# Seven block products in place of eight for a head pair's projections, block sums on GpSimd, buffers laid out anew

## The chip, the cores and the metric

The kernel runs on one core of a Trainium2 chip. The metric is the device time of one execution in microseconds. TensorE (PE) multiplies into PSUM; VectorE (DVE) and ScalarE (ACT) move results out of PSUM; GpSimd (POOL) works on SBUF only; transfers are issued by the queues of SyncE (SP), ACT and POOL. Each engine works through its own instructions in order, and waits on semaphores for the others.

## The reference, cut to what matters

A decoder block with three parts: a gated linear attention, a product with quantised operands, and a small block-diagonal feed-forward, each added to its input and normalised. The attention takes most of the time. In the reference it runs over blocks of 64 rows with a carried state; the kernel computes the same as one masked product over 512 rows, with a decay matrix.

```python
qkv = jax.nn.silu(hidden_states @ qkv_w.T)       # hidden: (2, 512, 1024), 32 heads of 128
scores = jnp.einsum('bhnd,bhmd->bhnm', cq, ck) * diag_decay
intra = jnp.einsum('bhnm,bhmd->bhnd', scores, cv)
...
xf = xf * jax.lax.rsqrt(jnp.mean(xf * xf, axis=-1, keepdims=True) + EPS)
normed = norm_w * xf.astype(attn.dtype)
gate = jax.nn.sigmoid(hidden_states @ gate_w.T)
return gate * normed @ out_w.T
```

Every float32 operand of these products is split into a high and a low float16 part, and a product is three: high x high, high x low, low x high.

## The kernel before, in words

`make_plan` writes one list of steps; five functions, one for each engine, walk that list and emit their part of each step. The order of the list is therefore the order of each engine's queue. Buffers are handed out by `Ring` objects that remember which semaphore value frees a slot.

The 32 heads form 16 groups of two. Groups 0 to 11 are worked for both batches in one block; groups 12 to 15 (`TAIL_GROUPS = 4`) once for batch 0 and then once for batch 1, so that batch 0's later stages run under batch 1's attention. In a block, each unit (a head h and a batch b) has these steps:

- `project` for q, k and the gate: 8 k-tiles of 3 matmuls of 128x512 into one bank (lines 779 to 781), 24 in all. For q and k, ACT takes the sigmoid of the bank (L947), DVE multiplies (L1074), ACT writes the high half (L950), DVE the low half (L1035): four turns of two engines. For the gate, ACT takes the sigmoid (L942).
- `project_v`, once for a group, a batch and 128 rows: 24 matmuls of 128x256 (L792 to L794), then the same four turns at half width.
- `scores`: 12 matmuls through the helper `three` (L762); DVE multiplies by the decay (L1087), ACT and DVE write the halves (L956, L1035), one bank after the other.
- `attend`: 12 matmuls (L817 to L819) into the one bank of `aring`; ACT squares (L962), DVE multiplies by norm weight and gate (L1100), ACT and DVE write the halves (L965, L1035), and DVE adds the square to `ssq` (L1106).
- `out_product` of the group before, for a batch and 128 rows: two halves of 6 matmuls each (L762), which DVE adds to `acc` (L1115).

Weights come by DMA from SP, 512 KB at a time, into five buffers `raw`; ACT writes the high half (L932) and DVE the low half (L1035). `between` inserts such steps between the projections. After the attention come `rows_phase` (residual, norm, quantised product) and `ffn_phase`.

## Time and profile before

| what | value |
|---|---|
| median of three runs | 2164.41 us (2163.93 to 2165.61) |
| the profiled execution | 2164.81 us, of which the span is 2162.9 us |
| PE busy | 2028.4 us (94%) |
| DVE busy | 1272.9 us (59%) |
| ACT busy | 816.1 us (38%) |
| POOL busy | 119.1 us (6%) |
| mean granted clock of TensorE | 0.97 |

Read it so: the page's share of busy time is a mean over the span; the table of stretches gives it by stage, with the granted clock beside it. Matmuls overlap each other in their records (one lasts longer than the step from one to the next), so what PE needs for a piece of work is read from the starts of the first and of the next piece in the timeline, not from durations. In a timeline row the first number is the start, the second the time to the end of the group of merged instructions, and in brackets stands how long the engine had been idle and who released it.

### The profile page before, as it was taken

How to read it: one execution, taken by the hardware profiler on the slowest of the kernel's cores; microseconds unless marked ns; L12 is line 12 of the kernel's file. 1: busy time of each engine (PE TensorE's matmuls, PEld its weight loads, DVE VectorE, ACT ScalarE, POOL GpSimd, SP SyncE). 2: the span in 40 equal slices, each digit the busy share in tenths (PEclk: the TensorE clock that was granted, in tenths of full speed). 3: DMA queues.
4: the chain of work that ended last, by engine and by line, in shares of the span. 5: the costliest groups of instructions: out<-in, count | busy, mean ns of one | idle time of the engine just before them, and what ended most of it. 6: DMA issues, size and time to landing. Idle time of an engine off the chain costs nothing.

```text
span 2162.9 us, 29130 instructions
## 1 busy us (share of the span) xinstructions
PE 2028.4 (94%) x11455; PEld 1098.8 (51%) x11464; DVE 1272.9 (59%) x1966; ACT 816.1 (38%) x1360; POOL 119.1 (6%) x132
## 2 busy tenths in 40 slices
PE   7999999999999999999999999999999899986654
PEld 4464646455564646464645555455555445542211
DVE  5655555555555555555555556556666666667887
ACT  4432323242323233332323233333444434444763
POOL 0000000000000000000000000000000000004465
PEclk9999999999999999999999999999999999997877
DMA  5120202020201102120202022123323322323311
GB/s 196 44 74 35 74 35 74 13 96 1 98 10 40 69 35 73 35 74 35 74 24 84 1 98 69 38 104 108 108 80 138 117 96 104 106 83 103 93 55 58
DMA packets 54071, 154.02 MB, mean 71 GB/s; under 512 B 5936, under 2 KB 14256, under 8 KB 53936
## 3 DMA queue, kind: packets, MB, share of 16 engines
q1 hardware_dynamic: 41056, 135.28, 17.8%
q0 software_dynamic: 3840, 12.59, 1.9%
q10 hardware_dynamic: 9040, 4.29, 0.7%
q8 instruction: 92, 1.51, 0.3%
q14 instruction: 43, 0.35, 0.1%
HBM read 143.75 MB, written 8.39 MB: 70 GB/s over the span
## 4 chain that ended last, share of the span: by engine, by line
PE 78%; DVE 11%; ACT 4%; issue 3%; DMA 2%; SPq 1%; POOL 1%; POOLq 0%; ACTq 0%; DVEq 0%
PE bank L762 18%; PE bank L781 14%; PE bank L780 14%; PE bank L779 14%; PE bank L792 4%; PE bank L794 4%; PE bank L793 4%; PE bank L817 1%; PE bank L819 1%; PE bank L818 1%; DVE x_split L1178 1%; DMA raw<-w_qk 1%; DVE w_head L1035 1%; DVE w_out_group L1183 1%; DVE bank L1087 1%
## 5 line engine op out<-in xcount | busy, mean ns | idle before, releaser
L779 PE MATMUL bank<-x_split,w_head 128*128 128x512 f16 x1536 | 582.7, 379 | 0.2 <-DVE v_split L1035 0.2
L780 PE MATMUL bank<-x_split,w_head 128*128 128x512 f16 x1536 | 582.6, 379 | 0.0
L781 PE MATMUL bank<-x_split,w_head 128*128 128x512 f16 x1536 | 582.4, 379 | 0.0
L762 PE MATMUL bank<-w_out_group,gated_split 128*128 128x512 f16 x1536 | 344.6, 385 | 20.8 <-DVE acc L1115 11.0
L947 ACT ACTIVATE sig<-bank 128x256 f32<-128x256 f32 (+1 forms) x256 | 124.8, 487 | 563.1 <-PE bank L781 496.9
L1074 DVE SCALAR_TENSOR_TENSOR bank<-bank,sig 128x256 f32<-128x256 f32 (+1 forms) x256 | 144.3, 564 | 273.7 <-ACT sig L947 272.3
L792 PE MATMUL bank<-w_v_group,x_split 128*128 128x256 f16 x1024 | 281.8, 275 | 18.9 <-DVE x_split L1035 11.4
L794 PE MATMUL bank<-w_v_group,x_split 128*128 128x256 f16 x1024 | 281.7, 275 | 0.0
L793 PE MATMUL bank<-w_v_group,x_split 128*128 128x256 f16 x1024 | 281.7, 275 | 0.0
L762 PEld LDWEIGHTS bank<-w_out_group,gated_split 128*128 128x128 f16 x1536 | 151.2, 99 | 209.1 <-issue 26.2
L781 PEld LDWEIGHTS bank<-x_split,w_head 128*128 128x128 f16 x1536 | 150.4, 98 | 181.3 <-issue 0.3
L779 PEld LDWEIGHTS bank<-x_split,w_head 128*128 128x128 f16 x1536 | 150.6, 98 | 169.3 <-DVE v_split L1035 0.5
L780 PEld LDWEIGHTS bank<-x_split,w_head 128*128 128x128 f16 x1536 | 150.4, 98 | 168.7
L1115 DVE TENSOR_TENSOR acc<-acc,bank 128x512 f32<-128x512 f32 x240 | 160.0, 685 | 86.4 <-PE bank L762 86.1
L1035 DVE SCALAR_TENSOR_TENSOR w_head<-raw,w_head 128x1024 f16<-128x1024 f32 x120 | 146.4, 1225 | 86.3 <-ACT w_head L932 86.1
L956 ACT ACTIVATE scores_split<-bank 128x512 f16<-128x512 f32 (+1 forms) x192 | 100.9, 526 | 249.7 <-DVE bank L1087 249.7
L1035 DVE SCALAR_TENSOR_TENSOR scores_split<-bank,scores_split 128x512 f16<-128x512 f32 (+1 forms) x192 | 115.8, 603 | 114.6 <-ACT scores_split L956 114.6
L1087 DVE TENSOR_TENSOR bank<-bank,decay_sb 128x512 f32<-128x512 f32 (+3 forms) x256 | 119.8, 491 | 34.9 <-PE bank L762 34.9
L932 ACT ACTIVATE w_head<-raw 128x1024 f16<-128x1024 f32 x120 | 125.4, 1051 | 37.8 <-DMA raw<-w_qk 37.6
L762 PE MATMUL bank<-q_split,k_split 128*128 128x512 f16 (+3 forms) x768 | 116.1, 302 | 2.7 <-DVE k_split L1035 2.7
L792 PEld LDWEIGHTS bank<-w_v_group,x_split 128*128 128x128 f16 x1024 | 100.9, 99 | 33.8 <-issue 10.0
L794 PEld LDWEIGHTS bank<-w_v_group,x_split 128*128 128x128 f16 x1024 | 101.1, 99 | 12.6
(172 smaller groups left out, 1987.6 us busy)
## 6 DMA issues: line engine op xcount, KB each, us to landing
raw<-w_qk SPq DMA_DIRECT2D x80, 512.0 KB, 4.6
raw<-w_v SPq DMA_DIRECT2D x40, 512.0 KB, 7.5
raw<-w_gate SPq DMA_DIRECT2D x40, 512.0 KB, 6.2
raw<-w_out SPq DMA_DIRECT2D x40, 512.0 KB, 4.5
decay_sb<-decay SPq DMA_DIRECT2D x40, 256.0 KB, 2.7
raw<-ctx_in SPq DMA_DIRECT2D x16, 512.0 KB, 4.6
acc<-x_t SPq DMA_DIRECT2D x8, 512.0 KB, 9.7
raw<-x_n SPq DMA_DIRECT2D x8, 512.0 KB, 4.2
```

What stands on the lines that cost most here:

```text
L762: last = pe.matmul(out, a, b, start=m == 1, stop=m == n)
L779: pe.matmul(bank[:, :], wt[:, j, 0, k], x[:, 0, k], start=k == 0, stop=False)
L780: pe.matmul(bank[:, :], wt[:, j, 0, k], x[:, 1, k], start=False, stop=False)
L781: mm = pe.matmul(bank[:, :], wt[:, j, 1, k], x[:, 0, k], start=False, stop=k == KT - 1)
L792: pe.matmul(out, x[:, 0, k, cols], c.w_vg[:, 0, k], start=k == 0, stop=False)
L793: pe.matmul(out, x[:, 0, k, cols], c.w_vg[:, 1, k], start=False, stop=False)
L794: mm = pe.matmul(out, x[:, 1, k, cols], c.w_vg[:, 0, k], start=False, stop=k == KT - 1)
L932: act.activation(hi, src, ACT.Copy, scale=scale).then_inc(sem["w_hi"])
L1035: return dve.scalar_tensor_tensor(out=lo, in0=src, scalar=scale, in1=hi, op0=ALU.mult, op1=ALU.subtract)
L1074: dve.scalar_tensor_tensor(out=ps, in0=ps, scalar=1.0 / W_SCALE, in1=c.sig32[st["gi"]][:, 0:n], op0=ALU.mult, op1=ALU.mult).then_inc(sem[" ...
L1087: ins = dve.tensor_tensor(ps, ps, c.decay_sb[slot][:, 0:n], ALU.mult)
L1115: dve.tensor_tensor(dst, dst, bank[:, :], ALU.add).then_inc(sem["acc"])
```

## The change

For groups 0 to 12 (`MAIN = 13`) the q, k and gate projections of a head pair are treated as a product of 2x2 blocks: two heads by two halves of the hidden size, times two halves by two batches. A block product is 4 k-tiles of 3 matmuls of 128x512. Instead of eight such products for each of q, k and gate, seven are made, of sums of blocks (the scheme of Winograd). What comes with it:

- The seven blocks of x are made once at the start: sums and differences of 128x2048 on DVE (`x_t1`, `x_t3`) and POOL (`x_t2`, `x_t4`), then a high and a low half of each (ACT and DVE, 128x2048 each). x arrives in four transfers of 1 MB.
- The weights of a pair arrive in one transfer of 1 MB into one of two buffers. POOL makes three block sums (and one in place) with four additions of 128x512 (`pair_sum`). ACT and DVE write the halves of 7 blocks of 512 columns in three parts, 1024, 1024 and 1536 wide (`pair_split`), where before there were two of 1024 for each of the three.
- The results are built up in PSUM. Product 1 goes to bank 0, ACT copies bank 0 to bank 1 (`seed`), and product 2 goes on in bank 0, product 6 in bank 1. Product 7 goes to bank 2 and ACT copies it to SBUF (`copy_p7`, `s7`). DVE adds bank 1 and `s7` into bank 2 (`u3`); product 5 goes on in bank 1; DVE adds bank 1 and `s7` into `s7` (`c22`); product 4 goes on in bank 2, product 3 in bank 1. The order on PE is 1, 7, 2, 6, 5, 4, 3. The four results are the four units of the pair; unit 3 is read from SBUF.
- v is still made with all its matmuls, but for a second batch the first half of k uses the block `b0 - b1`: ACT copies the first partial result (`v_copied`), DVE subtracts (`v_sub`), and PE waits for both.
- The scores, attends and out products of group n-1 are placed by hand into the products of group n: all scores and attends lie in the gate's products (the fourth attend in q's), all out products in q's, and the four v tiles in k's. The decays of the scores are taken one ahead of the low halves.
- The addition to `ssq` goes from DVE to POOL for these groups.
- `TAIL_GROUPS` is 3, and the steps from the main part to the tail are written out. The tail's own steps are as before; `between` advances `rows_phase` twice at a time, the second batch's x block is loaded again (`x12`), and most buffers of the tail are views of the main part's.

```diff
...
+PRODUCTS = {1: (0, 0, 0), 2: (1, 1, 0), 3: (6, 3, 1), 4: (3, 6, 2), 5: (2, 2, 1), 6: (4, 4, 1), 7: (5, 5, 2)}
...
+    def product(self, i):
...
+        free = {1: self.bank_free[0], 7: self.bank_free[2], 2: self.t_seeded, 6: self.t_seeded, 5: self.t_u3,
+                4: self.t_u3, 3: self.t_c22}[i]
...
+    plan.split_pair(0)
+    for name in ("x_t1", "x_t3", "x_t2"):
+        plan.add(name)
+        plan.tick(name)
+    for i, block in enumerate(X_ORDER):
+        plan.x_split(block)
+        if i == 0:
+            plan.split_pair(1)
+        if i == 1:
+            split_pair(2)
+        if block == 1:
+            plan.add("x_t4", split=plan.x_block[1])
+            plan.tick("x_t4")
+    plan.add("quant_consts")
+
...
+        fill("p1-")
+        plan.product(1)
+        fill("p1")
+        plan.seed()
+        fill("p7-")
+        plan.product(7)
+        plan.copy_p7()
+        fill("p7")
+        plan.product(2)
+        out(0)
+        fill("p2")
+        plan.product(6)
+        plan.add_u3()
+        fill("p6")
+        plan.product(5)
+        plan.add_c22()
+        out(3)
+        fill("p5")
+        plan.product(4)
+        fill("p4")
+        out(2)
+        plan.product(3)
+        fill("p3")
+
...
+        product_pair("gate", n, {
...
+            "p1-": [score(0)],
+            "p1": [part(0)],
+            "p7": [attend(0), score(1)],
+            "p2": [part(1)],
+            "p6": [attend(1), score(2)],
+            "p5": [part(2)],
+            "p4": [attend(2), score(3)],
+            "p3": [split_vo],
+        })
+        product_pair("q", n, {
+            "p1": gate_last if first else [attend(3)] + gate_last,
+            "p7": [part(0)],
+            "p6": [part(1)] if first else out(0, 1, 2, 3) + [part(1)],
+            "p5": [] if first else out(4, 5),
+            "p4": [part(2)] if first else [part(2)] + out(6, 7),
+            "p3": [lambda: plan.qk_out("q", 1)] + ([] if first else out(8, 9, 10, 11, 12, 13, 14, 15)),
+        })
+        if not first:
+            plan.load_decay(n * GH)
+            plan.load_decay(n * GH + 1)
+        product_pair("k", n, {
+            "p1": [split_vo],
+            "p2": [part(0)],
+            "p6": [lambda: plan.v_pair(0)],
+            "p5": [part(1)],
+            "p3": [lambda: plan.qk_out("k", 1), part(2), lambda: plan.v_pair(1), lambda: plan.v_pair(2),
+                   lambda: plan.v_pair(3)],
+        })
...
+    plan.main_scores(last_n, UNITS[0])
+    plan.finish_loads(plan.idle, ("head", g0 * GH))
+    plan.project(g0 * GH, 0, 0)
+    plan.main_attend(last_n, UNITS[0])
+    plan.main_scores(last_n, UNITS[1])
+    plan.prefetch_v(g0)
+    plan.project(g0 * GH, 0, 1)
...
+            i, wp = st["i"], st["wp"]
+            block, x, place = PRODUCTS[i]
+            bank, fresh = c.banks[place], i in (1, 7)
+            until(pe, sem, st["free"])
+            until(pe, sem, st["x"])
+            pe.wait_ge(sem["w_lo"], st["w"][1])
+            for k in range(QT):
+                w_hi, w_lo = (c.wp[:, wp, n, block, k * P:(k + 1) * P] for n in range(2))
+                x_hi, x_lo = (c.xb[:, x, n, k, :] for n in range(2))
+                pe.matmul(bank[:, :], w_hi, x_hi, start=fresh and k == 0, stop=False, skip_group_check=not fresh)
+                pe.matmul(bank[:, :], w_hi, x_lo, start=False, stop=False, skip_group_check=not fresh)
+                mm = pe.matmul(bank[:, :], w_lo, x_hi, start=False, stop=k == QT - 1, skip_group_check=not fresh)
...
+            pe.wait_ge(sem["v_copied"], st["copied"][1])
...
+            pe.wait_ge(sem["v_sub"], st["sub"][1])
...
+            act.activation(c.banks[1][:, :], c.banks[0][:, :], ACT.Copy).then_inc(sem["seeded"])
...
+            act.activation(c.s7[:, :], c.banks[2][:, :], ACT.Copy).then_inc(sem["p7_copied"])
...
+            dve.tensor_tensor(bank[:, :], c.banks[1][:, :], c.s7[:, :], ALU.add).then_inc(sem["u3"])
...
+            dve.tensor_tensor(c.s7[:, :], c.banks[1][:, :], c.s7[:, :], ALU.add).then_inc(sem["c22"])
...
+            until(pool, sem, st["free"])
+            pool.wait_ge(sem[st["landed"][0]], st["landed"][1])
+            pool.tensor_tensor(s3, a11, a21, ALU.add)
+            pool.tensor_tensor(a21, a21, a22, ALU.add).then_inc(sem["pair_sum"])
+            pool.wait_ge(sem["pair_sum"], st["s1"][1])
+            pool.tensor_tensor(s2, a11, a21, ALU.add).then_inc(sem["pair_sum"])
+            pool.wait_ge(sem["pair_sum"], st["s2"][1])
+            pool.tensor_tensor(s4, a12, s2, ALU.add).then_inc(sem["pair_sum"])
+        elif kind == "x_t2":
...
+            pool.tensor_tensor(c.ssq[:, b], c.ssq[:, b], c.square_of(st), ALU.add).then_inc(sem["ssq_pool"])
...
```

## Rows read from the trace of the kernel before

**Rows 1.** Table of stretches: us, each engine's busy time (instructions), clock, DMA share, GB/s.
```profile
1150.00:1200.00 50.00, 50.00 (x346) 33.22 (x345) 25.15 (x44) 18.68 (x37) 0.00 (x0) 1.00 0.23 80
```

**Rows 2.** Timeline of PE, group 4: start, us, engine line op, names, count.
```profile
613.25 1.79 PE L762 MATMUL bank<-q_split,k_split 128*128 128x512 f16 x12
614.88 0.38 PE L779 MATMUL bank<-x_split,w_head 128*128 128x512 f16 x1
...
620.06 2.11 PE L762 MATMUL bank<-w_out_group,gated_split 128*128 128x512 f16 x9
```

**Rows 3.** Timeline of ACT: sigmoids of the last two v tiles at the start.
```profile
36.79 0.38 ACT L947 ACTIVATE sig<-bank 128x256 f32<-128x256 f32 x1 [1.35 <-PE bank L794]
...
39.41 0.38 ACT L947 ACTIVATE sig<-bank 128x256 f32<-128x256 f32 x1 [1.36 <-PE bank L794]
```

**Rows 4.** Timeline of DVE: one addition of half an out product.
```profile
637.09 0.69 DVE L1115 TENSOR_TENSOR acc<-acc,bank 128x512 f32<-128x512 f32 x1 [0.61 <-PE bank L762]
```

**Rows 5.** Timeline of ACT: first v sigmoid of two successive groups.
```profile
596.22 0.38 ACT L947 ACTIVATE sig<-bank 128x256 f32<-128x256 f32 x1
...
713.19 0.38 ACT L947 ACTIVATE sig<-bank 128x256 f32<-128x256 f32 x1
```

**Rows 6.** Timelines of ACT and DVE: the four turns of one q.
```profile
646.16 0.60 ACT L947 ACTIVATE sig<-bank 128x512 f32<-128x512 f32 x1 [23.41 <-PE bank L781]
646.79 0.70 DVE L1074 SCALAR_TENSOR_TENSOR bank<-bank,sig 128x512 f32<-128x512 f32 x1 [5.12 <-ACT sig L947]
647.52 0.60 ACT L950 ACTIVATE q_split<-bank 128x512 f16<-128x512 f32 x1 [0.77 <-DVE bank L1074]
648.15 0.69 DVE L1035 SCALAR_TENSOR_TENSOR q_split<-bank,q_split 128x512 f16<-128x512 f32 x1 [0.66 <-ACT q_split L950]
```

**Rows 7.** Groups of instructions by line: busy us, mean ns, idle before.
```profile
L1035 DVE SCALAR_TENSOR_TENSOR w_head<-raw,w_head 128x1024 f16<-128x1024 f32 x120 | 146.4, 1225 | 86.3 <-ACT w_head L932 86.1
L932 ACT ACTIVATE w_head<-raw 128x1024 f16<-128x1024 f32 x120 | 125.4, 1051 | 37.8 <-DMA raw<-w_qk 37.6 <-DMA raw<-w_gate 0.2
```

**Rows 8.** Timelines of ACT and DVE: square and low half of one attend.
```profile
690.79 0.59 ACT L962 ACTIVATE square<-bank 128x512 f32<-128x512 f32 x1
...
692.95 0.69 DVE L1035 SCALAR_TENSOR_TENSOR gated_split<-bank,gated_split 128x512 f16<-128x512 f32 x1 [0.66 <-ACT gated_split L965]
```

**Rows 9.** Timeline of DVE: later decays of one unit's scores.
```profile
660.84 0.76 DVE L1087 TENSOR_TENSOR bank<-bank,decay_sb 128x384 f32<-128x384 f32 x2
...
662.86 0.42 DVE L1087 TENSOR_TENSOR bank<-bank,decay_sb 128x256 f32<-128x256 f32 x1
```

**Rows 10.** Timelines of DVE and ACT at the start: splits of x.
```profile
13.44 7.31 DVE L1035 SCALAR_TENSOR_TENSOR x_split<-acc,x_split 128x512 f16<-128x512 f32 x12
18.09 1.15 ACT L936 ACTIVATE x_split<-acc 128x512 f16<-128x512 f32 x2 [0.20 <-DMA acc<-x_t]
```

**Rows 11.** Timelines of POOL and DVE in the feed-forward stage.
```profile
2049.33 1.06 POOL L1247 TENSOR_TENSOR square<-acc 128x512 f32<-128x512 f32 x1
...
2051.54 1.27 POOL L1252 TENSOR_TENSOR sig<-sig,square 128x512 f32<-128x512 f32 x1
2048.98 4.39 DVE L1178 TENSOR_TENSOR x_split<-w_head,x_split 64x512 f16<-64x512 f32 x1
```

**Rows 12.** Timeline of PE: the stop where both-batch blocks end.
```profile
1328.37 11.81 PE L762 MATMUL bank<-w_out_group,gated_split 128*128 128x512 f16 x54 [1.42 <-DVE acc L1115]
```

**Rows 13.** Timeline of PE, two stops, and the stretches behind each.
```profile
1931.03 1.19 PE L762 MATMUL bank<-q_split,k_split 128*128 128x512 f16 x3 [2.74 <-DVE k_split L1035]
1932.00:1934.00 2.00, 2.00 (x11) 1.30 (x10) 0.92 (x3) 1.01 (x1) 0.00 (x0) 0.50 0.23 23
1934.00:1936.00 2.00, 2.00 (x9) 0.83 (x8) 0.76 (x1) 1.17 (x3) 0.00 (x0) 0.81 0.65 242
1942.76 0.38 PE L817 MATMUL bank<-scores_split,v_split 128*128 128x512 f16 x1 [2.20 <-issue]
1942.00:1944.00 2.00, 1.24 (x7) 0.71 (x8) 0.57 (x2) 2.00 (x4) 0.00 (x0) 1.00 0.00 0
```

747 lines of the change are left out of this document (598 added, 149 removed).

## The prediction

> **What bounds the kernel now.** I read the table of stretches first. In the main part PE is busy for all 50 us of a 50 us stretch at granted clock 1.00 (the full level of 2.4 GHz), DVE for about half [rows 1]. Then the waits of PE: between 60 and 1300 us that view is empty. So in groups 0 to 11 only matmuls cost time; every wait that the change adds to PE there counts in full, and so does every matmul that it takes away.
>
> What PE needs, from starts in the timelines: a projection of 24 matmuls takes 620.06 - 614.88 = 5.18 us, so 0.216 us a matmul and 2.59 us for a block product of 12. Scores take 614.88 - 613.25 = 1.63 us, an attend with the same column counts as much [rows 2]. A v tile takes 39.41 - 36.79 = 2.62 us [rows 3]; half an out product 0.69 + 0.61 = 1.30 us [rows 4]. A group: 12 x 5.18 + 8 x 2.62 + 8 x 1.63 + 16 x 1.30 = 117 us, and the same step recurs after 713.19 - 596.22 = 117.0 us [rows 5]. PE has no slack.
>
> **Matmuls removed.** 3 kinds x 12 matmuls = 36 a group, 36 x 0.216 = 7.8 us, for 13 groups -101 us. A group then needs 117.0 - 7.8 = 109.2 us of PE. This is sure; the question is what is given back.
>
> **The steady group (1 to 12).** Prices: the four turns of a q or k result start 0.63, 0.73, 0.63 us apart (sigmoid, product, high half, low half; the last slot 0.61), 2.6 us together, because each engine waits for the other [rows 6]. A low half of 1024 takes 1.23 us on DVE and the high half 1.05 on ACT; 0.69 and 0.60 are those of 512 [rows 6, 7], so 1536 is estimated at 1.76 and 1.5. An attend holds DVE from its gate product on for 0.75 + 0.6 + 0.7 = 2.0 us, 2.8 us after the square begins [rows 8]. A score block is 0.68 and 0.35 [rows 9] and 0.61 [rows 10] of decays and as much of low halves, 3.3 us on DVE in the new order. I lay these behind each other in the written order, PE's start of the gate's products being 0:
> - Gate part. PE has 7 x 2.59 + 7 x 1.63 = 29.5 us. DVE has 4 x 3.3 of scores, 3 x 2.0 of attends, 4.0 of splits, 1.3 of `u3` and `c22`, and 1.9 left over from the last v tile, plus waits for ACT: it falls behind. The low halves of the fourth scores come at 32.8, PE wants the fourth attend at 32.1: 0.8 us.
> - q part. ACT's order is `split_vo`, square, high half, `gate_out(1)`, `seed`. The fourth attend ends on PE at 34.6; DVE comes from `split_vo` at 36.0; gate product, high half, gate and seed follow to 38.4. Product 2 waits for the seed from 37.2: 1.3 us. Here and in k, out products and v tile 0 cover `u3`, and product 4 covers `c22`.
> - End of the k part. Products 5, 4 and 3 follow each other without filler, and three results with two parts of a split go through ACT and DVE in turns. With T the end of product 3 on PE: `c22` from T-5.0, unit 3 until T-1.7, the split of part 1 until T-0.1, unit 2 until T+1.8, unit 1's high half until T+3.2, the 1536-wide high half until T+4.6, and only then ACT's copy of v tile 1, until T+4.9. PE wants it at T+2.6 and stops for 2.4 us; then `v_sub` is late by another 0.4, behind the 1536-wide low half.
>
> Together 0.8 + 1.3 + 2.4 + 0.4 = 4.9 us, and 0.5 for the starts after four stops: 5.4 us of 7.8. For 12 groups +65 us. No row shows these stops. Bounds: 3.0 us (only the k part) gives +36, 7.5 (a third more of everything) +90. I take 5.4, since each of its turns has a row of the same shape. No gain is possible here: PE had no wait to lose.
>
> **Group 0 and the start.** In the q and k parts of group 0 nothing fills the places: `u3` stands open (1.2), bank 2 is late (0.6), the k end as above: +5 us (3 to 7). At the start the kernel of before has its first v products done at 39.4 us for 8 x 2.62 = 21.0 us of work [rows 3]: 18.4 us lost. The last 512 KB of x land at about 18 us [rows 10], after 5 MB as in the change. In the change ACT's seed of the first product stands in its queue behind the high halves of all seven x blocks. Block 6 waits for `x_t4` on POOL, and that for block 1's low half. A DVE pass of 2048 is estimated at 2.3 us (0.61 per 512 in a row [rows 10], 1.23 per 1024), one of POOL at 4.9 (1.22 to 1.27 per 512 [rows 11]). DVE: `x_t1` 12.8 to 15.1, `x_t3` to 17.8, then block 0, part 1, block 5, part 2, block 1 to 27.2; `x_t4` to 32.3; high halves of 6 and 3 to 36.1; seed 36.7. Five products, `u3` and a half clock at first (below) end at 53; ideal is 18.1. Lost 35, that is +17. With POOL and DVE excluding each other, as next, it ends at 61: +25. I take +21, bounds 14 and 28.
>
> **POOL beside DVE.** At 2048.98 a DVE operation with both inputs in SBUF, 0.69 us otherwise, takes 4.39: POOL's operations run back to back until 2052.8 and DVE ends 0.56 us behind them [rows 11]. Under the same burst DVE operations with an input in PSUM kept their length. The pair's sums are bursts of 4 x 1.27 = 5.1 us, three a group; what can be hit are the weight splits and unit 3. By my layout one burst meets q's part 0 split (5 us of out products cover it), the others run beside v tiles and out additions, whose inputs are in PSUM. In the steady group 0. The Trainium skill, page "SBUF — State Buffer", section "Who interferes with whom", says that a VectorE instruction with two SBUF inputs and a GpSimd one that reads SBUF exclude each other for a whole instruction. The row agrees, and goes further: POOL's operations in a row held DVE out. By the rule alone, with one operation of 1.27 a hit and two hits a group, the sum would be at most 12 x 2.5 = 30 higher, and only where nothing covers the split.
>
> **From main part to tail.** After the last v tile PE has one score block (1.6 us), then waits for three splits: DVE's scores end at 5.1, three low halves at 9.1: 7.6 us idle. The v weights' splits stand behind the third attend and fourth scores: about 6.5. The out weights' splits stand behind the v tiles: about 3. Sum 17, and 4 for the clock: +21 (14 to 26). The before had one stop of 1.4 us at its own passage [rows 12], which goes: -1.4.
>
> **The tail.** The second batch's part, under which batch 0's row steps and the context hide, is one block shorter; its extra work is the same. -5 to +12, I take +4. Transfers are no bound: a pair's 1 MB has about 30 us.
>
> **The clock.** The stop of 2.74 us was followed by the level of 1.2 GHz: after 2.74 us of idle, 2 us at 0.50 and 2 us at 0.81 lose 1.4 us, with what lay before them some 1.7; after 2.20 us the clock stayed at 1.00 [rows 13]. The new stop of 2.4 us lies between. I take it as mostly unhurt, +3 us in all (0 to 22).
>
> **Sum.** -101 + 65 + 5 + 21 + 21 - 1.4 + 4 + 3 = +16.6. 2162.9 + 16.6 = 2179.5 of span; the execution was 1.9 us longer than its span, and it stands 0.4 us above the median of the runs: 2181 us, 0.8% slower.
>
> **The rivals.**
> - The k end is not late (faster). Mechanism and place: ACT's copy of v tile 1. It decides at 2.6 us behind product 3. If the chain of turns runs 2.4 us ahead of my layout, because unit 3 and part 1 are done before product 4 ends, then 2.8 us a stop vanish 13 times, the 3 us of clock too: 2181 - 39 = 2142. With the gate part's stops gone as well (2.1 x 12), 2117. For it: in the rows of before the same turns never stop PE, and a part of my durations overlaps in the records. Against: in before no two results came closer than 5.18 us, here 2.59. Chance 0.28.
> - The clock falls at every k end (slower). 13 x 1.7 = 22 in place of 3, and 3 to 5 in the start: 2203. For it the 2.74 us row, against it the 2.20 one. Chance 0.14.
> - POOL's bursts reach the gate part. If a pair's sums start beside the third or fourth scores, a split is held for what is left of 5.1 us, some 3 on average, with no cover [rows 11]; 12 x 3 = 36: 2217. Against: they stand in POOL's queue behind the fourth `ssq`. Chance 0.08.
> - The change doesn't do what it says: matmuls that go on in a bank written by ACT or DVE step slower than 0.216. No row shows such a bank. At 0.22 it would be 13 x 180 x 0.004 = 9 us: 2190. Chance 0.02.
> - The forecast as worked out: 0.48, its own range 2160 to 2200.
>
> **How the numbers follow.** The likeliest case gives 2181. The range takes the first rival's nearer time with room, 2130, and the POOL rival's, 2217. About 0.2% (4 us, to 2160 and 2169) is what a measurement of this kernel can tell from no change. Faster takes the first rival and a little of the forecast's low bounds: 0.30. The same: 0.11. Slower: 0.59.
>
> **What would show it.** In the changed kernel PE's waits from 100 to 1400 us must name three places, the attend behind the fourth scores, the seed before product 2, and ACT's copy and DVE's difference in v tile 1, with 5 us a group together and a period near 114.5 us. A period under 111 speaks for the first rival. Clock rows of 0.5 to 0.9 once a group speak for the clock, DVE splits of 3 to 6 us in the gate part for POOL. The first group's products should end at 53 to 61 us. The prediction is wrong if PE hardly waits there, or if the passage to the tail costs far from 20 us.

## The result and the profile after

The changed kernel takes 2178.28 us (median of 4 runs, 2176.79 to 2179.55), the kernel before 2164.17 us beside it (2162.66 to 2165.61): a ratio of 1.0065, 95% interval [1.0048, 1.0082]. It is slower by 0.65%. The profiled execution has a span of 2176.8 us, 13.9 more than before, and a mean granted clock of 0.962.

The matmuls did go. The page of the changed kernel, instructions and busy time of each engine:

```profile
PE 1955.0 (90%) x10988; PEld 1057.4 (49%) x10997; DVE 1388.8 (64%) x2068; ACT 934.5 (43%) x1512; POOL 434.0 (20%) x342
```

PE has 10988 matmuls where it had 11455: 467 fewer (13 x 36 = 468, one record may be missing), and is busy for 90% of the span where it was for 94%. What it lost is in the waits. Waits of PE, changed kernel, whole span (us in total, times, longest), and in a second block the same view from 200 to 1300 us, where the kernel before has no wait at all:

```profile
PE bank L1220 <- ACT bank L1447: 28.2, 14, 11.1
PE bank L1246 <- ACT sig L1460: 25.0, 12, 2.1
```

```profile
PE bank L1246 <- ACT sig L1460: 20.9, 10, 2.1
PE bank L1220 <- ACT bank L1447: 12.2, 9, 1.4
PE bank L1312 <- issue: 4.7, 9, 0.5
PE bank L1253 <- DVE bank L1616: 1.4, 4, 0.4
```

L1246 is the third of the four stages of a v tile (it waits for ACT's copy, L1460), L1253 the fourth (for DVE's difference, L1616), L1220 a product (for the seed, L1447), L1312 an attend. They stand at fixed places of each group. Timeline of PE, changed kernel, one group: start, us, what ran, and in brackets the idle time before it and its releaser:

```profile
223.57 0.28 PE L1246 MATMUL bank<-w_vo,x_blocks 128*128 128x256 f16 x1 [2.09 <-ACT sig L1460]
225.42 0.40 PE L1253 MATMUL bank<-w_vo,x_blocks 128*128 128x256 f16 x1 [0.26 <-DVE bank L1616]
...
271.39 0.38 PE L1312 MATMUL bank<-scores_split,v_split 128*128 128x512 f16 x1 [0.52 <-issue]
...
277.13 0.39 PE L1220 MATMUL bank<-x_blocks,w_pair 128*128 128x512 f16 x1 [1.36 <-ACT bank L1447]
...
339.05 0.28 PE L1246 MATMUL bank<-w_vo,x_blocks 128*128 128x256 f16 x1 [2.09 <-ACT sig L1460]
...
1373.38 0.28 PE L1246 MATMUL bank<-w_vo,x_blocks 128*128 128x256 f16 x1 [2.09 <-ACT sig L1460]
```

The same stop recurs after 339.05 - 223.57 = 115.5 us. In group 0 it is at 108.31, in group 11 at 1373.38: (1373.38 - 108.31) / 11 = 115.0 us a group, where it was 117.0 [rows 5] and 109.2 of matmuls are left.

Why the v tile waits is on ACT and DVE. Timeline of ACT ahead of that stop, changed kernel (the 1536-wide row is part 2 of the next pair's split), then the two rows of DVE:

```profile
219.80 0.59 ACT L1465 ACTIVATE sig<-bank 128x512 f32<-128x512 f32 x1
221.27 0.60 ACT L1470 ACTIVATE k_units<-bank 128x512 f16<-128x512 f32 x1 [0.87 <-DVE bank L1620]
221.76 1.47 ACT L1432 ACTIVATE w_pair<-sums_pair 128x1536 f16<-128x1536 f32 x1
223.14 0.38 ACT L1460 ACTIVATE sig<-bank 128x256 f32<-128x256 f32 x1
...
223.27 1.76 DVE L1570 SCALAR_TENSOR_TENSOR w_pair<-sums_pair,w_pair 128x1536 f16<-128x1536 f32 x1 [0.68 <-ACT w_pair L1432]
224.94 0.42 DVE L1616 TENSOR_TENSOR bank<-sig,bank 128x256 f32<-128x256 f32 x1
```

ACT has unit 1's turn and then part 2 ahead of the copy (L1460), with no idle time but the 0.87 in which it waits for DVE inside the turn. The copy ends at 223.52; PE starts at 223.57. The clock is the other thing that appears. Table of stretches, changed kernel (length, then PE, PEld, DVE, ACT, POOL busy, clock, DMA share, GB/s), behind the stops of two successive groups:

```profile
224.00:226.00 2.00, 1.74 (x13) 1.13 (x12) 1.75 (x3) 0.38 (x1) 0.89 (x1) 0.70 0.00 0
226.00:228.00 2.00, 2.00 (x12) 1.41 (x10) 0.47 (x2) 0.39 (x1) 1.92 (x3) 0.50 0.89 262
228.00:230.00 2.00, 2.00 (x19) 1.76 (x18) 0.86 (x2) 1.15 (x3) 1.92 (x2) 0.95 0.64 262
...
342.00:344.00 2.00, 2.00 (x21) 1.79 (x19) 1.00 (x3) 1.03 (x3) 1.92 (x2) 1.00 0.94 350
```

After the same 2.09 us of idle the level of 1.2 GHz (0.50) appears in one group and not in the next. It appears after 8 of the 12 stops. A period that begins with a fall is 115.3 to 115.5 us long, one without is 114.1, so a fall costs 1.1 to 1.4 us here. The clock itself loses more in the three rows, 0.30 x 2 + 0.50 x 2 + 0.05 x 2 = 1.7 us; part of that is covered, because behind a fall PE comes to DVE's difference later and waits for it less or not at all, where it waits 0.37 us in a group without a fall.

The start and the passage to the tail. Timeline of PE, changed kernel: the first products, and the passage:

```profile
23.21 0.61 PE L1220 MATMUL bank<-x_blocks,w_pair 128*128 128x512 f16 x1 [20.33 <-DVE x_blocks L1570]
...
42.15 0.61 PE L1220 MATMUL bank<-x_blocks,w_pair 128*128 128x512 f16 x1 [11.09 <-ACT bank L1447]
...
1507.62 0.58 PE L1274 MATMUL bank<-x_blocks,w_pair 128*128 128x512 f16 x1 [7.46 <-DVE w_pair L1570]
1541.28 0.37 PE L1287 MATMUL bank<-w_vo,x_blocks 128*128 128x256 f16 x1 [6.22 <-DVE w_vo L1570]
```

11.09 us is the wait for the first seed, behind the x splits. The third gap of the passage is 3.07 us (at 1560.42).

So the 101 us of removed matmuls, and 14 more, were given back in four places: steady stops, the start, the passage and the clock. What the runs had to settle is whether each stop is what the prediction said it is: an engine's queue ahead of one operation, which can be reordered, or a chain that has to be that long.

### The profile page after: what moved, and what is told of

It is laid out like the page before. It is cut to its first block, busy times and chain, and to the rows that moved or that the text cites. A ratio compares the mean times of both kernels' runs of the same rounds, so it can differ in the third digit from the quotient of the medians.

```text
span 2176.8 us, 29088 instructions
## 1 busy us (share of the span) xinstructions
PE 1955.0 (90%) x10988; PEld 1057.4 (49%) x10997; DVE 1388.8 (64%) x2068; ACT 934.5 (43%) x1512; POOL 434.0 (20%) x342
## 4 chain that ended last, share of the span: by engine, by line
PE 73%; DVE 14%; ACT 6%; issue 5%; DMA 1%; POOL 1%; SPq 0%; ACTq 0%; POOLq 0%; DVEq 0%
PE bank L1197 18%; PE bank L1220 10%; PE bank L1222 10%; PE bank L1221 10%; PE bank L1274 2%; PE bank L1276 2%; PE bank L1275 2%; DVE w_pair L1570 2%; PE bank L1312 2%; ACT w_pair L1432 1%; PE bank L1314 1%; PE bank L1313 1%; DVE x_blocks L1570 1%; PE bank L1253 1%; PE bank L1254 1%
## 5 line engine op out<-in xcount | busy, mean ns | idle before, releaser
L1220 PE MATMUL bank<-x_blocks,w_pair 128*128 128x512 f16 x1092 | 415.8, 381 | 51.9 <-ACT bank L1447 28.2
L1221 PE MATMUL bank<-x_blocks,w_pair 128*128 128x512 f16 x1092 | 415.7, 381 | 0.0
L1222 PE MATMUL bank<-x_blocks,w_pair 128*128 128x512 f16 x1092 | 415.5, 381 | 0.0
L1197 PE MATMUL bank<-w_vo,gated_split 128*128 128x512 f16 x1152 | 256.5, 379 | 0.0
L1833 POOL TENSOR_TENSOR ssq<-ssq,sig 128x512 f32<-128x512 f32 x52 | 86.0, 1654 | 575.1 <-ACT sig L1497 575.1
L1220 PEld LDWEIGHTS bank<-x_blocks,w_pair 128*128 128x128 f16 x1092 | 107.2, 98 | 181.0 <-ACT bank L1447 35.1
L1570 DVE SCALAR_TENSOR_TENSOR w_pair<-raw_pair,w_pair 128x1024 f16<-128x1024 f32 x108 | 141.5, 1317 | 71.6 <-ACT w_pair L1432 58.5
L1620 DVE SCALAR_TENSOR_TENSOR bank<-bank,sig 128x256 f32<-128x256 f32 (+1 forms) x182 | 99.2, 545 | 135.0 <-ACT sig L1465 134.4
L1814 POOL TENSOR_TENSOR sums_pair<-raw_pair 128x512 f32<-128x512 f32 x39 | 51.6, 1323 | 645.8 <-DVE w_pair L1570 400.3
L1197 PEld LDWEIGHTS bank<-w_vo,gated_split 128*128 128x128 f16 x1152 | 112.7, 98 | 135.9
L1222 PEld LDWEIGHTS bank<-x_blocks,w_pair 128*128 128x128 f16 x1092 | 107.2, 98 | 130.0 <-issue 1.9
L1465 ACT ACTIVATE sig<-bank 128x256 f32<-128x256 f32 (+1 forms) x182 | 86.2, 474 | 191.4 <-PE bank L1248 112.7
L1221 PEld LDWEIGHTS bank<-x_blocks,w_pair 128*128 128x128 f16 x1092 | 107.2, 98 | 119.6 <-issue 1.8
L1491 ACT ACTIVATE scores_split<-bank 128x512 f16<-128x512 f32 (+1 forms) x192 | 100.7, 526 | 119.3 <-DVE bank L1673 115.3
L1274 PE MATMUL bank<-x_blocks,w_pair 128*128 128x512 f16 x288 | 112.0, 389 | 15.7 <-DVE w_pair L1570 15.7
L1276 PE MATMUL bank<-x_blocks,w_pair 128*128 128x512 f16 x288 | 111.7, 388 | 0.0
L1275 PE MATMUL bank<-x_blocks,w_pair 128*128 128x512 f16 x288 | 111.6, 388 | 0.0
L1197 PE MATMUL bank<-k_units,gated_split 128*128 128x512 f16 x384 | 89.7, 393 | 13.5 <-DVE acc L1705 6.2
L1570 DVE SCALAR_TENSOR_TENSOR w_pair<-sums_pair,w_pair 128x1536 f16<-128x1536 f32 (+1 forms) x45 | 75.8, 1684 | 37.3 <-ACT w_pair L1432 35.7
```

What stands on the lines that cost most here:

```text
L1197: last = pe.matmul(out, a, b, start=m == 1, stop=m == n)
L1220: pe.matmul(bank[:, :], w_hi, x_hi, start=fresh and k == 0, stop=False, skip_group_check=not fresh)
L1221: pe.matmul(bank[:, :], w_hi, x_lo, start=False, stop=False, skip_group_check=not fresh)
L1222: mm = pe.matmul(bank[:, :], w_lo, x_hi, start=False, stop=k == QT - 1, skip_group_check=not fresh)
L1274: pe.matmul(bank[:, :], wt[:, j, 0, k], x_hi, start=k == 0, stop=False)
L1275: pe.matmul(bank[:, :], wt[:, j, 0, k], x_lo, start=False, stop=False)
```

## Experiments

Each starts from the changed kernel ("p4" is the place behind product 4 in the list of a projection's fillers, and so on); `...` marks cut lines. Ratios are against the kernel before, and "less" or "more" is against the changed kernel's 2178.28 us. The theory: the k end's stop is ACT's queue ahead of v tile 1's copy; the gains and losses of the places add up. Its rival: the stop is a chain that moves but does not shrink.

**k_end: v tile 1 ahead of unit 1's turn.**

```diff
-            "p3": [lambda: plan.qk_out("k", 1), part(2), lambda: plan.v_pair(1), lambda: plan.v_pair(2),
-                   lambda: plan.v_pair(3)],
+            "p3": [lambda: plan.v_pair(1), lambda: plan.qk_out("k", 1), part(2), lambda: plan.v_pair(2),
+                   lambda: plan.v_pair(3)],
```

> At the end of each k part v tile 1 is placed ahead of unit 1's result and of part 2 of the split; nothing else changes. Order theory (the stop of 2.09 us at v tile 1 and the 0.37 behind it come from ACT's place in its queue, and the half clock in two of three groups from the length of that stop): ACT's copy of v tile 1 then follows unit 2's high half at 1.2 us behind product 3 and is in time, both stops go, the clock stays at 1.00, and the period falls from 115.26, 115.48, 114.13 us to about 111.6 in every group. 13 x (2.1 + 0.3) + 9 x 1.25 = 43 us less than 2178: 2135 us. Rival (GpSimd's sums delay VectorE and through it the k end): the stop keeps most of its length, 2165 us or more. Rival (matmuls in banks that ACT or DVE wrote are slower): no change, 2178.

Measured 2179.43 us, ratio 1.0057 [1.0037, 1.0078]: no gain, a miss. The trace shows where the stop went. Timelines of ACT and then PE, k_end:

```profile
226.45 0.59 ACT L1465 ACTIVATE sig<-bank 128x512 f32<-128x512 f32 x1
227.81 0.60 ACT L1470 ACTIVATE k_units<-bank 128x512 f16<-128x512 f32 x1 [0.77 <-DVE bank L1620]
228.30 1.48 ACT L1432 ACTIVATE w_pair<-sums_pair 128x1536 f16<-128x1536 f32 x1
229.67 0.38 ACT L1460 ACTIVATE sig<-bank 128x256 f32<-128x256 f32 x1
...
230.10 0.28 PE L1246 MATMUL bank<-w_vo,x_blocks 128*128 128x256 f16 x1 [2.23 <-ACT sig L1460]
```

These are the same three pieces of work, now ahead of v tile 2's copy, and PE stops for 2.23 us one tile later. The queue was the cause, but I had moved it, not shortened it: v tiles follow each other without a filler, so whatever stands between two of their copies stops PE. The time alone, 2179, would also have fitted the rival in which matmuls are slower in banks that ACT or DVE wrote. The starts of the products in the changed kernel rule that out: products 5 and 4 of a gate part, in such banks, take 262.26 - 257.08 = 5.18 us, products 1 and 7, in fresh banks, 245.38 - 240.20 = 5.18.

**k_split_late: part 2 of the split behind the last v tile.**

```diff
-            "p3": [lambda: plan.qk_out("k", 1), part(2), lambda: plan.v_pair(1), lambda: plan.v_pair(2),
-                   lambda: plan.v_pair(3)],
+            "p3": [lambda: plan.qk_out("k", 1), lambda: plan.v_pair(1), lambda: plan.v_pair(2),
+                   lambda: plan.v_pair(3), part(2)],
```

> Only part 2 of the split is moved, behind all four v tiles; unit 1's result stays ahead of v tile 1. This tells which turn in the chain is dear. The copy of v tile 1 then comes after unit 1's high half, 3.6 us behind product 3 in place of 4.9: the stop falls from 2.1 to about 0.8 and the clock no longer falls: 13 x 1.7 + 9 x 1.25 = 33 us gained. But the 1.76 us of VectorE and then GpSimd's sums of the next pair move to the beginning of the gate part, where by the layout VectorE has no slack: the stop at the fourth attend grows from 0.5 to 2.3, and q's part 0 split may wait for a burst. 12 x 1.8 to 12 x 2.8 lost. Net -11 to 0: 2167 to 2178 us. If VectorE has slack in the gate part after all, 2145.

Measured 2157.92 us, ratio 0.9957 [0.9943, 0.9971]: 20.4 us less than the changed kernel, and faster than before. Waits of PE from 200 to 1300 us, k_split_late:

```profile
PE bank L1312 <- issue: 9.6, 20, 0.5
PE bank L1246 <- ACT sig L1460: 7.2, 10, 0.7
```

The stop fell from 2.09 to 0.72, by 1.37 (part 2's slot on ACT is 223.14 - 221.76 = 1.38). The difference's wait is gone. Two small stops are new (0.39 for part 2's low half, 0.43 for an attend). The clock stays at 1.00 in this run's groups. The period is 113.4, from 115.0: 1.6 x 12 = 20, nearly the whole gain. The time lies between the two that I gave: the k end did what was expected, but my main case had the fourth attend's stop grow to 2.3 us by DVE's extra 1.76 us, and it stayed at 0.53. At the beginning of the gate part DVE had room for that piece.

**ssq_dve: the addition of the squares back on DVE.** In the branch of DVE for an attend, and the same taken out of POOL's:

```diff
             if "unit" in st:
+                dve.wait_ge(sem[st["ssq_before"][0]], st["ssq_before"][1])
+                dve.tensor_tensor(c.ssq[:, b], c.ssq[:, b], c.square_of(st), ALU.add).then_inc(sem["ssq_pool"])
                 continue
...
```

> Undoes one part of the change: the addition to ssq of groups 0 to 12 is VectorE's again. Order theory with VectorE as the one that sets the gate part: 0.61 us more for each of four attends there, of which some 0.6 are absorbed by slack before the second and third attend; the stop at the fourth attend grows from 0.5 by about 1.5 and q's seed stays where it is behind it: 12 x 1.5 to 12 x 2.2, so 2196 to 2205 us. Rival (the GpSimd addition holds the splits, its mean is 1.65 us against 1.27 alone, so moving it costs as much as it saves): 2178 or less.

Measured 2222.20 us, ratio 1.0250 [1.0233, 1.0267]: 44 us more, beyond both. Waits of PE from 200 to 1300 us, ssq_dve; then the split of v's and out's weights on DVE in one group, in the changed kernel and in ssq_dve, and POOL beside the latter:

```profile
PE bank L1220 <- ACT bank L1447: 28.0, 9, 3.5
PE bank L1312 <- issue: 15.1, 9, 1.7
```

```profile
272.25 2.36 DVE L1570 SCALAR_TENSOR_TENSOR w_vo<-raw_pair,w_vo 128x1024 f16<-128x1024 f32 x2 [0.96 <-ACT w_vo L1437]
...
277.44 4.25 DVE L1570 SCALAR_TENSOR_TENSOR w_vo<-raw_pair,w_vo 128x1024 f16<-128x1024 f32 x2 [0.96 <-ACT w_vo L1437]
280.70 2.13 POOL L1821 TENSOR_TENSOR sums_pair<-raw_pair,sums_pair 128x512 f32<-128x512 f32 x1
```

The k end's stop is as it was (2.09). The attend's stop grows from 0.52 to 1.67, by 1.15, the direction and nearly the size that was expected (about 1.5): three of the four additions stand ahead of the fourth scores in DVE's queue. What I had wrong is the seed, which was to stay: its stop grows from 1.36 to 3.1 in the mean. The rows say why. The pair's sums on POOL now meet `split_vo` on DVE, whose two pieces take 4.25 us together in place of 2.36. In the group in which one piece alone is held (1.22 and 2.29 us, at 396.56) the seed's stop is 2.43; in the group shown, with both held, it is 3.25, and 3.25 - 1.36 = 1.89 is the time for which POOL held the two. So of the 2.9 us a group, 35 in 12, more than half comes from POOL holding DVE and not from the additions' own length; the rest of the 44 us is not worked out, but behind the seed's stop the clock now falls too in some groups (0.50 from 286 to 288 us), for which I had no term. This is the prediction's rival of POOL's bursts; in the changed kernel the additions of squares on POOL stood ahead of the sums and kept them off that split.

**eight: product 4 made twice.** 12 more matmuls a projection, so as many as before, everything else as in the changed kernel. The output is not the reference's: block 3's product counts twice.

```diff
-            for k in range(QT):
+            for m in range(QT * (2 if i == 4 else 1)):
+                k, last = m % QT, m == QT * (2 if i == 4 else 1) - 1
...
```

> Product 4 is made twice in each of the 39 pairs' products, which puts back the number of matmuls of an eighth product (the result is then not the reference's). 39 x 2.59 = 101 us of matmuls more. Order theory: during 2.59 us more of cover the copy of v tile 1 and q's fourth scores catch up, so the stops at the k end (2.4), the clock falls (0.85 a group on average) and most of the stops at the fourth attend (0.5) and the seed (1.4) go: 13 x 3.2 + 12 x 1.9 = 65 us come back, 2178 + 36 = 2214 us, so an eighth of the products costs a third of its price. Rival (the stops are independent of cover): 2279 us.

Measured 2240.48 us, ratio 1.0339 [1.0321, 1.0356]: 62 us more for 101 us of matmuls, between the two: 39 us came back where I expected 65. The period went from 115.0 to 119.7, 7.8 of matmuls and -3.1 of the rest: the attend's 0.52 is gone, the seed's 1.36 is 0.81, the v tile's 2.09 is 1.08, and the clock does not fall in any of these groups. So the stops are not a fixed price of the new order; part of them is time in which the other engines catch up, and matmuls put there cost less than their length. This measures directly what the seven products bring inside this kernel: 62 us, not 101.

**k_p4: part 2 ahead of unit 2's turn.**

```diff
+            "p4": [part(2)],
-            "p3": [lambda: plan.qk_out("k", 1), part(2), lambda: plan.v_pair(1), lambda: plan.v_pair(2),
+            "p3": [lambda: plan.qk_out("k", 1), lambda: plan.v_pair(1), lambda: plan.v_pair(2),
```

> Whole computation; only the k part's last piece (1536 wide, 1.47 on ACT and 1.76 on DVE) is moved ahead of product 3 of k instead of behind the last unit's silu. If v tile 1 waits for what is queued ahead of its copy on ACT (our theory), product 3's 7.8 us hide the piece together with unit 2's turn, the stop at v tile 1 falls from 2.09 to about 0.7 (only the last unit's turn is left ahead of the copy, as in the variant that put the piece last), the 0.39 that that variant waited for its next weights does not appear, and the clock does not fall: period 115.0 -> about 112.9, some 25 us in all, 2150 to 2156. Rival: the piece now delays unit 2's turn and its sums from GpSimd are not ready there, so that product 3's end meets a longer queue: the stop stays near 2 and the time near 2178.

Measured 2186.16 us, ratio 1.0096 [1.0078, 1.0115]: worse, a miss. The step that failed is the cover: I took 7.8 us for a product; that is three products, one takes 2.59. The stop is 2.62 us, and the clock falls to 0.50 behind 11 of these 12 stops (226 to 228 us in this group). Timeline of PE, k_p4:

```profile
224.85 0.28 PE L1247 MATMUL bank<-w_vo,x_blocks 128*128 128x256 f16 x1 [2.62 <-ACT sig L1461]
```

ACT's order brought nothing while the sum ahead of the copy stayed (k_end, k_p4); the piece has to leave the stretch of products 5, 4 and 3 altogether.

**k_spread: part 2 behind the last v tile, and part 1 out of that stretch too.**

```diff
-            "p6": [lambda: plan.v_pair(0)],
-            "p5": [part(1)],
-            "p3": [lambda: plan.qk_out("k", 1), part(2), lambda: plan.v_pair(1), lambda: plan.v_pair(2),
-                   lambda: plan.v_pair(3)],
+            "p6": [part(1), lambda: plan.v_pair(0)],
+            "p3": [lambda: plan.qk_out("k", 1), lambda: plan.v_pair(1), lambda: plan.v_pair(2),
+                   lambda: plan.v_pair(3), part(2)],
```

> Whole computation; as in the variant that moved k's last piece (1536 wide) behind v tile 3, and the middle piece (1024 wide, 1.04 on ACT, 1.23 on DVE) moved from behind product 5 of k to ahead of v tile 0, where ACT is free for 1.0 and DVE for 6 us. Products last 2.6 us each (12 matmuls x 0.216), so that between the end of product 5 and v tile 1's copy ACT has two units' turns of some 2.1 us each and the middle piece. Theory (the stop at v tile 1 is ACT's queue): without the middle piece unit 2's turn ends a microsecond earlier and the copy follows the last unit's turn alone: the stop 0.72 falls to 0 to 0.1, 13 x 0.7 = 9 us less than the 2157.9 of that variant: 2147 to 2151. Rival: the copy is bound by the last unit's own turn (sigmoid, product, high half, some 2.1 us from the end of product 3), which no other work lengthens: the stop stays 0.7 and the time 2158.

Measured 2146.00 us, ratio 0.9908 [0.9891, 0.9924]: as expected, 1 us below the range given. Waits of PE from 200 to 1300 us, k_spread, and under them its timeline of ACT ahead of the copy:

```profile
PE bank L1219 <- ACT bank L1446: 13.6, 10, 1.4
PE bank L1311 <- issue: 9.5, 20, 0.5
```

```profile
218.14 0.60 ACT L1464 ACTIVATE sig<-bank 128x512 f32<-128x512 f32 x1 [0.47 <-PE bank L1221]
219.50 0.60 ACT L1469 ACTIVATE k_units<-bank 128x512 f16<-128x512 f32 x1 [0.77 <-DVE bank L1619]
220.00 0.38 ACT L1459 ACTIVATE sig<-bank 128x256 f32<-128x256 f32 x1
```

No v tile waits any more (besides these two the view has only the 0.4 us for part 2's low half). ACT now waits for PE (0.47) ahead of unit 1's sigmoid, where in the changed kernel it had none: it has caught up with product 3. The rival, a chain that is bound by the last unit's own turn, falls. Period 112.5.

**start, passage, q_seed: one place each.** Start: the x blocks 6 and 3 are split behind group 0's first `u3` in place of ahead of its seed, and the split of q's first weights follows later.

```diff
-    for i, block in enumerate(X_ORDER):
+    for i, block in enumerate(X_ORDER[:5]):
...
-            "p1": [part(0)],
-            "p2": [part(1)],
-            "p5": [part(2)],
+            "p6": [late_x],
+            "p4": [part(0), part(1)],
+            "p3": [part(2)],
```

> Whole computation; x blocks 6 and 3 are split after group 0's first U3 in place of before the gate products, and q's first two pieces wait for that. Theory: the first seed waits behind those splits on ACT (11.09 us stop at 42.15), so that it comes earlier by the time of two 3.7 us ACT pieces, and part of it is lost again at the later products that read blocks 6 and 3: a gain of 3 to 9 us, 2170 to 2175 where the variant without it has 2178. Rival: GpSimd's sums and VectorE's wide low halves (which take 3.3 in place of 1.27 and 6.6 in place of 2.28 together) set the start whatever their order: 2178 within 2.

Measured 2170.79 us, ratio 1.0028 [1.0018, 1.0038]: 7.5 us less, as expected. The wait of 11.09 us for the seed is gone (3.08 and 2.94 later in its place).

Passage: the loads and splits of the tail's first head weights stand between group 12's v tiles.

```diff
+            "p3": [lambda: plan.qk_out("k", 1), lambda: plan.v_pair(1), tail_loads, tail_head, tail_split,
+                   lambda: plan.v_pair(2), tail_split, lambda: plan.v_pair(3), tail_split],
...
```

> Whole computation; at the end of the last seven-product group the tail's head weights are loaded and split between that group's v tiles instead of behind them. Theory: of the passage's gaps 7.5, 6.2 and 3.1 us the first is the wait for these splits and goes, perhaps some of the second: 6 to 12 us less, 2166 to 2172. Rival: the loads can't start earlier (the buffers that they write are read by products until then), the gap stays: 2178 within 2.

Measured 2169.55 us, ratio 1.0026 [1.0016, 1.0037]: 8.7 us less, as expected. Timeline of PE, passage:

```profile
1503.91 0.38 PE L1289 MATMUL bank<-x_blocks,w_pair 128*128 128x512 f16 x1 [2.02 <-DVE w_pair L1585]
1535.60 0.37 PE L1302 MATMUL bank<-w_vo,x_blocks 128*128 128x256 f16 x1 [6.21 <-DVE w_vo L1585]
```

The first gap is 2.02 us in place of 7.46; the first matmul behind it takes 0.38 where it took 0.58: the granted clock is 1.00 here, and was 0.50 from 1508 to 1510 us in the changed kernel. At the second gap this kernel is 5.7 us ahead; the rest of the gain comes later in the tail, and I have no row that says why.

q_seed: `split_vo` moves from the end of the gate part to behind product 7 of q.

```diff
-            "p3": [split_vo],
+            "p3": [],
...
-            "p7": [part(0)],
+            "p7": [part(0)] if first else [split_vo, part(0)],
```

> Whole computation; the split of v's and out's weights (2 pieces on ACT and DVE) is moved from the end of the gate part to behind product 7 of q, out of the queue ahead of the seed of q. Theory: the stop of 1.36 us ahead of product 2 of q becomes about 0.7 (one gate turn is still ahead of the seed), 12 x 0.65 = 8 us less: 2169 to 2173. Rival: the seed waits for the gate turn alone and the moved pieces now delay the out additions: 2178 or up to 5 us more.

Measured 2176.60 us, ratio 1.0058 [1.0041, 1.0074]: 1.7 us less, which the two intervals don't tell from nothing; 2169 to 2173 was expected, a miss. The seed's stop did halve. Waits of PE from 200 to 1300 us, q_seed, then the moved pieces on DVE and the first out product behind them:

```profile
PE bank L1220 <- ACT bank L1447: 6.1, 9, 0.7
PE bank L1197 <- issue: 4.9, 9, 0.6
```

```profile
275.49 4.37 DVE L1570 SCALAR_TENSOR_TENSOR w_vo<-raw_pair,w_vo 128x1024 f16<-128x1024 f32 x2 [1.92 <-ACT w_vo L1437]
...
279.97 4.26 PE L1197 MATMUL bank<-w_vo,gated_split 128*128 128x512 f16 x19 [0.55 <-issue]
```

The wait of the out products (L1197) is new, 0.55 us. They read the weights that these pieces split, and start 0.1 us behind them. The two pieces take 4.37 us for the 2.36 of the changed kernel, because at their new place they meet the pair's sums on POOL (272.74 to 278.78). With their own length they would have ended 2 us earlier, ahead of the out product: so by these rows what the seed won was lost to POOL.

**all_moves: the four moves together** (k_spread, start, passage, q_seed).

> Whole computation; the moves of the start, of the passage, of v's and out's weight split and of both of k's late pieces together. If each gain is a stop of its own, they add up: 2178.3 - 20.4 (k's last piece) - 9 (the middle one) - 7.5 (start) - 8.7 (passage) - 1.7 (weight split) = 2131, range 2125 to 2140: below the kernel before by 1.2 to 1.8%. Rival: a stop removed at one place comes back at the next (as when v tile 1 was put first): 2145 to 2155.

Measured 2133.26 us, ratio 0.9849 [0.9832, 0.9865]: 1.5% faster than the kernel before, and as expected. The single gains from the changed kernel's 2178.3 are 32.3, 7.5, 8.7 and 1.7, together 50.2; found are 45.0. They add up to within 5 us. Here too the moved pieces of `split_vo` take 4.37 us and the out products wait for 0.55; a run that keeps the pair's sums off them was not made.

**all_moves_vo_early: the out weights' split ahead of q's pair.** In the order of loads `("o", n - 1)` goes ahead of `("q", n)`, and in the gate part:

```diff
-            "p1": [part(0)],
+            "p7-": [split_vo],
             "p7": [attend(0), score(1)],
-            "p2": [part(1)],
-            "p6": [attend(1), score(2)],
+            "p2": [part(0)],
+            "p6": [attend(1), score(2), part(1)],
...
```

> Whole computation; as all moves together, but the out weights are loaded and split ahead of q's pair: their two pieces (2.0 on ACT, 2.36 on DVE) stand behind the gate seed, where DVE was idle for 2.4, and not in q. Theory: the seed of q waits for the gate turn alone (1.36 -> 0.7) and the 0.54 to 0.6 that the out products waited for when the split stood in q don't appear: 12 x 0.6 = 7 us less than all moves: 2124, range 2118 to 2134. Rival: the pieces of q's pair, now later in the gate part, hold up product 1 or 7 of q or the third attend: as all moves or up to 8 us more.

Measured 2153.89 us, ratio 0.9943 [0.9927, 0.9960]: 21 us more than all_moves, far beyond both. Waits of PE from 200 to 1300 us, all_moves_vo_early; then DVE ahead of the first gate product in all_moves, and two rows of DVE in all_moves_vo_early:

```profile
PE bank L1328 <- issue: 28.0, 20, 2.4
```

```profile
237.76 0.76 DVE L1705 SCALAR_TENSOR_TENSOR bank<-bank,norm_w_sb,gate_units 128x512 f32<-128x512 f32 x1 [0.78 <-ACT sig L1514]
...
237.64 2.36 DVE L1586 SCALAR_TENSOR_TENSOR w_vo<-raw_pair,w_vo 128x1024 f16<-128x1024 f32 x2 [0.98 <-ACT w_vo L1453]
...
253.75 1.23 DVE L1586 SCALAR_TENSOR_TENSOR w_pair<-raw_pair,w_pair 128x1024 f16<-128x1024 f32 x1 [0.47 <-ACT w_pair L1448]
```

The fourth attend's stop went from 0.52 to 2.37, and the clock falls behind 7 of the 12. The idle of 2.4 us was a row of the changed kernel (247.84); in all_moves, where k's late piece stands ahead of the gate part, DVE is idle for 0.78 and 0.47 us there. Even so the two pieces of `split_vo` are the lesser part: counted from the first decay, the second gate product comes 14.60 us behind it for 14.31 in all_moves, 0.3 later. The greater part is the last row: q's part 1, which had to make room, stands behind the third scores, where all_moves has no split, and takes 1.7 us of DVE with the idle before it. The fourth scores come 2.0 us later in all. That is the rival as recorded, the pieces of q's pair, at more than twice its price. The out products' wait did vanish, and `split_vo` is not held by POOL (2.36).

**x_sums_dve: the two 2048-wide sums of x on DVE,** on top of all_moves: `x_t2` behind block 0's split and `x_t4` behind the fifth block's, both issued by DVE in place of POOL.

> Whole computation; as all moves together (2133.3), with the two 2048-wide sums of x blocks made on VectorE in place of GpSimd, the first behind block 0's low half, the second behind the fifth block's. Theory: at the start GpSimd and VectorE take turns, not beside each other: GpSimd's 6.5 us sum stands beside block 0's low half, which then takes 6.60 in place of 2.28, and so the first product comes at 23.6. On VectorE the sums cost 2.3 each and nothing waits behind GpSimd: the low half ends 4.3 earlier and the first product starts at 19 to 20; of that 3 to 6 us reach the end of group 0: 2127 to 2130. Rival: the low half is late for another reason (its block's landing, the memory), and 2 x 2.3 more on VectorE lengthen the start: 2134 to 2140.

Measured 2130.77 us, ratio 0.9853 [0.9836, 0.9869], the span of the profiled execution 2127.5. The ratio is that of all_moves, so the gain of 3 to 6 us that was expected is not shown in the whole time; at the start it is. Timelines of POOL and DVE of all_moves, then of DVE and POOL of x_sums_dve:

```profile
14.82 6.54 POOL L1840 TENSOR_TENSOR k_units<-q_units,acc 128x2048 f32<-128x2048 f32 x1 [2.41 <-DMA acc<-x_t]
16.92 6.60 DVE L1587 SCALAR_TENSOR_TENSOR x_blocks<-acc,x_blocks 128x2048 f16<-128x2048 f32 x1
```

```profile
16.86 2.28 DVE L1588 SCALAR_TENSOR_TENSOR x_blocks<-acc,x_blocks 128x2048 f16<-128x2048 f32 x1
19.07 2.29 DVE L1619 TENSOR_TENSOR k_units<-q_units,acc 128x2048 f32<-128x2048 f32 x1
...
26.44 9.86 POOL L1842 TENSOR_TENSOR sums_pair<-raw_pair 128x512 f32<-128x512 f32 x1 [14.08 <-DVE w_pair L1588]
```

The same low half takes 2.28 in place of 6.60 us, and the first product starts at 19.21 in place of 23.58. At the first product 7 of group 1 the kernel is 119.66 - 114.31 = 5.35 us ahead.

## Why the prediction came out as it did

The forecast was 2181 us, slower; 2178.28 was measured. Its span of 2179.5 stands against 2176.8. By its own steps:

- **Matmuls, -101.** 467 fewer in the trace; held.
- **Steady group, 5.4 us a group.** 115.0 - 109.2 = 5.8 was measured, 66 us over 12 groups (the last has no k-end stop) against 65. The places are those that were named, with 0.52 for 0.8 (attend), 1.36 for 1.3 (seed), 2.09 for 2.4 (copy) and 0.26 to 0.38 for 0.4 (difference, but in 5 of 12 groups only). The turns of [rows 6] and the widths of [rows 7] laid end to end in the written order gave each within some 0.3 us. The stops are 4.1 us a group where I had 4.9; falls of the clock make up 0.8, and 0.9 no view names, where I had 0.5 for the starts. My 1536-wide estimates, 1.5 and 1.76, are 1.47 and 1.76 in the trace. k_split_late, k_spread and eight show that the k end is that queue, as the step says.
- **Group 0 and the start, +5 and +21.** The gate's products end at 59.6 us, in the 53 to 61 that I gave and near the end that goes with POOL and DVE excluding each other, which x_sums_dve then showed. The last v tile ends near 1498.5 (1507.62 - 7.46 - 1.63 for a score block); its matmuls are 13 x 109.2 less group 0's missing scores, attends and out products (8 x 1.63 + 16 x 1.30 = 33.8), 1385.8. Of the 112.7 lost, 66 are the steady stops and 46.7 the start and group 0, where I had 18.4 + 21 + 5 = 44.4.
- **POOL beside DVE, 0 in the steady group.** Held for the sum, but not because they never meet: the additions of squares take 2.35 and 1.85 us in the gate part where 1.27 is their length alone, and the pair's last sum 2.13. There POOL waits for DVE, and POOL is on no path. The one hit on DVE that I had laid out is there: q's part 0 takes 2.06 us for 1.23 in every group, and the out products cover it. How near the other case was, ssq_dve and q_seed show: with one step moved, the sums hold `split_vo` for 1.9 to 2.0 us.
- **Passage, +17 and 4.** Gaps 7.46, 6.22 and 3.07 for 7.6, 6.5 and 3.
- **Tail, +4.** What is left of the 13.9: 13.9 + 101.1 - 66 - 28.3 - 16.8 + 1.4 = 5.3, which holds the passage's clock too, where I had 8.
- **The clock, +3.** Too small, and the one term of the sum that was off by a factor, of three. 2.09 us of idle were followed by the lower level in 8 of 12 groups; [rows 13] with 2.74 and 2.20 had let me place it on the safe side. At 1.2 us a time that is some 10 us, hidden in the 5.8 of the period, beside shorter stops than I had laid out. Two errors of some 7 us (the clock) and 8 us (the stops) cancelled here: that the sum comes within 3 us of the measured span is luck to that extent.

The rivals: the k end not late (2142) is refuted, the stop is there 12 times. POOL's bursts in the gate part did not show in the changed kernel (they do in ssq_dve). The clock's rival was half right: it named the place and the 1.7 us that a fall loses, but 8 falls of 12, of which each lengthens the period by some 1.2 us. Matmuls in a bank that ACT or DVE wrote step at the same pace: 24 of them in 5.18 us, as in [rows 2].

Why it is slower at all: eight says that the seven products are worth 62 of their 101 us here, and the start and the passage that came with them cost 45 (28.3 and 16.8). What kept it from winning is the order of the steps, not the method: with four moves it is 1.5% faster than before. Whether the kernel before would gain by moves of its own was not tried; between 60 and 1300 us its PE had no wait to lose.

## What to carry to other kernels

When PE has no slack, price a saving by the queue that each following operation stands in: lay the turns of the two slower engines end to end in the written order, with a time for each from a row, and compare with the (now shorter) time that PE gives them. Then ask of each piece in that queue whether it must be there; a reorder that keeps the sum ahead of the operation that PE wants moves the stop and saves nothing (k_end, k_p4), taking a piece out of the stretch saves its length as long as a stop is left to shorten (k_split_late, k_spread). Read the idle time that is to take the piece in the trace of the very kernel that you change, and price the pieces that must make room with the same care as the one that you move (all_moves_vo_early). Then look at what POOL does beside the new place: a split of two SBUF inputs that meets its sums takes nearly twice its length (ssq_dve, q_seed).

## What the runs showed of the hardware

- **POOL and DVE held each other for whole operations, and by either's order.** In the changed kernel DVE's low half of 2048 took 6.60 us beside a POOL sum of 6.54, and 2.28 without it. In x_sums_dve it was POOL's turn: its 512-wide sum, 1.27 alone, took 9.86, from 26.44 to 36.30, and DVE's four 2048-wide operations in a row ended at 35.2. In [rows 11] POOL in a row had held DVE. In other places the two took turns one by one: in the changed kernel from 36.9 to 46.8 us three of POOL's sums take 3.2 to 3.3 us each and two of DVE's low halves 3.35, and in ssq_dve DVE's pieces took 2.04 and 2.29 for 1.23. The Trainium skill, page "SBUF — State Buffer", section "Who interferes with whom", says that a VectorE instruction with two SBUF inputs contends with a GpSimd instruction that reads SBUF, for a lock that one of them holds alone. The traces agree; the runs add that the wait can last for several operations of the other engine in a row. What decides between that and turns stays open.
- **The same stop of 2.09 us was followed by the level of 1.2 GHz in 8 of the changed kernel's 12 groups,** with the same instructions ahead of it each time. Counted in the same way in the other runs, between 100 and 1480 us: after the same 2.09 us 8 of 12 in start and in passage, 7 in q_seed and 5 in ssq_dve; after stops of 2.23 us (k_end) 8 of 12, of 2.37 (all_moves_vo_early) 7 of 12, of 2.62 (k_p4) 11 of 12. After the stops of 1.36 us (changed kernel, k_end, k_split_late, k_spread, k_p4) and of 1.67 (ssq_dve) the clock did not fall once, 72 stops in all, nor in eight and all_moves, whose stops in the groups are shorter. What decides between 2.09 and 2.62 stays open.
